# Two-layer graph network: the row of a node's mean from an on-chip table instead of a widened x; the dense pass beside the second and third mean pass

## The reference, cut to what matters

```python
def _sage_conv(x, src, dst, Wl, bl, Wr):
    summed = segment_sum(x[src], dst, N_NODES)
    cnt = segment_sum(ones, dst, N_NODES)
    mean = summed / maximum(cnt, 1.0)[:, None]
    return mean @ Wl.T + bl + x @ Wr.T
h = relu(_sage_conv(x, src, dst, Wl0, bl0, Wr0))
h = relu(_sage_conv(h, src, dst, Wl1, bl1, Wr1))
h = _sage_conv(h, src, dst, Wl2, bl2, Wr2)
x = layernorm(x + h)
# second layer: softmax attention of each edge over its source node
q, k, v = (x @ Wq)[src], (x @ Wk)[dst], (x @ Wv)[dst]
attn = einsum(q, (k + edges @ Wek) * scale) @ W_exp
attn = softmax of attn over the edges of one src
agg  = segment_sum(attn * (v + edges @ Wev), src)
x = layernorm(x + (x @ Wv - agg) @ W_out)
```

## Time and profile before

| | us |
|---|---|
| median of 3 runs | 3042.29 |
| lowest and highest | 3033.99, 3043.68 |
| span of the profiled execution | 3046.9 |

### The profile page before, as it was taken

How to read it: one execution, slowest core, us unless ns; L and a number is a source line. 1 busy time by engine, 2 the same in 40 slices (tenths; PEclk the granted TensorE clock), 3 DMA queues, 4 the chain that set the end, 5 groups by cost and what they waited for, 6 DMA issues and landing times.

```text
span 3046.9 us, 39880 instructions
## 1 busy us (share of the span) xinstructions
PE 1807.8 (59%) x8855; PEld 1270.6 (42%) x8855; DVE 1508.0 (49%) x4640; ACT 937.6 (31%) x2157; POOL 2059.0 (68%) x2154
## 2 busy tenths in 40 slices
PE   0159938994555556666666664777777777772000
PEld 0135525663444445544444443455555555551000
DVE  6767836883222223332333333577776776773000
ACT  0025524441111111112222221455655565552000
POOL 0037777776656557767777777777777777773776
PEclk9999969996777778787887876888988898986555
DMA  8954426886899967876434332344544445443221
GB/s 270 343 171 139 144 89 181 237 229 161 159 199 185 185 144 150 146 133 182 116 114 121 118 109 76 89 135 135 146 131 141 131 135 141 135 137 95 91 88 60
DMA packets 464252, 448.74 MB, mean 147 GB/s; under 512 B 62929, under 2 KB 342370, under 8 KB 464134
## 3 DMA queue, kind: packets, MB, share of 16 engines
q1 hardware_dynamic: 335558, 285.34, 30.9%
q0 software_dynamic: 62720, 110.02, 19.7%
q10 hardware_dynamic: 65856, 52.20, 5.2%
HBM read 285.01 MB, written 168.95 MB: 149 GB/s over the span
## 4 chain that ended last, share of the span: by engine, by line
POOL 39%; issue 27%; DMA 14%; PE 8%; DVE 8%; SPq 2%; POOLq 1%; ACT 1%; DVEq 0%; ACTq 0%
POOL GX L601 17%; POOL hsrc L601 10%; DMA dsti<-in_dst_dram 6%; POOL out_dram L677 4%; POOL x_with_lookup L616 4%; POOL x_prime L677 3%; DMA GX<-in_x_dram,idx_a 2%; PE bank L733 2%; PE bank L788 2%; DVE hsrc L1130 2%; DMA GX<-x_with_lookup,idx_a 1%; DVE hsrc L1131 1%; PE bank L792 1%; DMA GX<-mean_product,idx_a 1%; DMA x_prime<-normed,idx_b 1%
## 5 line engine op out<-in xcount | busy, mean ns | idle before, releaser
L601 POOL DMA_INDIRECT GX<-mean_product,idx_a x392 | 404.6, 1032 | 121.4 <-issue 109.2
L1265 DVE TENSOR_TENSOR_SCAN seg<-flag,seg,hsrc 128x512 f32<-128x512 f32 x147 | 188.7, 1284 | 523.0 <-ACT hsrc L975 421.6
L788 PE MATMUL bank<-h,wt 128*128 128x512 f32 x588 | 325.2, 653 | 0.8 <-ACT h L947 0.4
L825 PE MATMUL bank<-hsrc,wt 128*128 (+1 forms) x196 | 150.2, 858 | 254.4 <-ACT hsrc L975 134.0
L733 PE MATMUL bank<-ident,hsrc 128*128 128x128 f32 (+1 forms) x466 | 93.3, 336 | 320.0 <-DMA hsrc<-x_prime,idx_d 174.8
L733 PE MATMUL bank<-ident,GX 128*128 128x128 f32 x588 | 107.8, 313 | 286.2 <-DMA GX<-in_x_dram,idx_a 176.0
L601 POOL DMA_INDIRECT hsrc<-x_prime,idx_d x196 | 215.3, 1099 | 84.4 <-issue 44.8
L601 POOL DMA_INDIRECT hsrc<-x_prime,idx_c x196 | 209.8, 1070 | 59.7 <-issue 58.5
L601 POOL DMA_INDIRECT GX<-x_with_lookup,idx_a x196 | 209.9, 1071 | 58.8 <-issue 55.0
L677 POOL DMA_INDIRECT x_prime<-normed,idx_b x196 | 196.3, 1002 | 66.7 <-issue 63.8
L953 ACT ACTIVATE logv<-mv,eps 128x4 f32<-128x4 f32 x294 | 86.9, 296 | 487.7 <-DVE mv L1235 486.1
(11 more groups left out here) (164 smaller groups left out, 4403.4 us busy)
## 6 DMA issues: line engine op xcount, KB each, us to landing
flag<-same_dst_row SPq DMA_DIRECT2D x147, 256.0 KB
mean_product<-prod SPq DMA_DIRECT2D x147, 256.0 KB
hsrc<-mean_product SPq DMA_DIRECT2D x147, 256.0 KB, 3.7
x_with_lookup<-hsrc ACTq DMA_DIRECT2D x98, 264.0 KB, 4.6
hsrc<-in_x_dram ACTq DMA_DIRECT2D x98, 256.0 KB, 4.6
XN<-in_x_dram SPq DMA_DIRECT2D x98, 256.0 KB, 3.0
x_prime<-normed SPq DMA_DIRECT2D x98, 256.0 KB
XN<-x_prime SPq DMA_DIRECT2D x98, 256.0 KB, 4.8
```

The costliest lines, as they stand in the source:

```text
L601: pool.indirect_dma_start(buf[:, c.slot(U), t, 0:width], None, table, bass.IndirectOffsetOnAxis(ap=idx[:, c.slot(U), t:t + 1], axis=0)).th ...
L788: last = pe.matmul(psum[:, :], wt[:, T_R[i], :], before[:, c.slot(2), :], start=True, stop=not dst_phase)
L825: pe.matmul(psum[:, :], wt[:, T_R[i], :], take_cols(hsrc, c.index() * CH, CH), start=True, stop=False)
L1265: dve.tensor_tensor_scan(seg[:, c.slot(2), :], flag[:, c.slot(4), :], take_cols(hsrc, c.index() * CH, CH), seg[:, before.slot(2), CH - 1:C ...
```

## The change

1. **No widened tables.** `x_with_lookup`, `edge_attr_with_dst`, the phase lk and all that fed them are gone; mean0 gathers from x itself, attend from the edge values themselves.
2. **Marks.** During the sort ACT makes, for each of 200 columns of 125 destinations, two tiles of signs (256 and 196 wide, bf16), and PE sums their products in two banks, 400 matmuls in all (`mark`): a table of how many destinations lie below a node. 44 marks stand ahead of the first turn of the sort, up to 10 after each turn, and what is left (65) behind the turned indices. 8 buffers of marks.
3. **The table.** DVE and PE make from it `node_table`: for a node, the position of its mean, or a row of zeros (`make_table`, `table_sums`, put in by `run`'s new `middle`).
4. **Look-up in mean0.** For each chunk, DVE makes one-hot rows of the low byte (`look_hot_rows`), PE multiplies them by the table (`look_up`, 16 matmuls bf16 of 196), DVE picks by the high byte (`look_take`, 4 operations with a sum) and writes `lookup`. The mean part runs 6 chunks (`LAG`) ahead of it.
5. **Look-up in dst** of an edge's destination, in the same way, 8 matmuls bf16 of 256 and 4 picks of 256 a chunk, for `idx_d` of attend, whose wait and cast go.
6. **The dense pass** moves: chunks 0 to 48 beside mean1, 49 to 97 beside mean2, none beside mean0.
7. mean0's first gather waits only for the first turned list.

The core of the diff:

```diff
-            run(pe, "dense", chain, FIRST, to_end=False)
...
+            def look_up(c):
+                pe.wait_ge(look_hot.of(c), look_hot.after(c))
+                pe.wait_ge(look_done.of(c), look_done.after(c, 2 if c.phase == "mean0" else 1))
...
+                for t in range(TPC):
+                    to = bank[look_banks(c)[t // 2]][:, t % 2 * width:(t % 2 + 1) * width]
+                    for k, (rows, table) in enumerate(pairs):
+                        last = pe.matmul(to, rows[:, t * P:(t + 1) * P], table, start=k == 0, stop=k == len(pairs) - 1)
+                last.then_inc(look_sum.of(c), 1)
...
-                    run(pe, "mean0", [(3, second(chain_t), SECOND), (3, mean_turn), (2, second(chain_1), SECOND),
-                                      (1, mean_prod), (1, second(chain_2), SECOND), (0, second(chain_y), SECOND)], NC)
+                    run(pe, "mean0", [(LAG + 1, mean_turn), (0, look_up), (LAG, mean_prod)], NC, middle=table_sums)
+                    look_done.end(pe, "mean0")
                 else:
-                    run(pe, f"mean{i}", [(1, mean_turn), (0, mean_prod)], NC)
+                    dense = first if i == 1 else second
+                    run(pe, f"mean{i}", [(3, dense(chain_t)), (1, mean_turn), (2, dense(chain_1)),
+                                         (0, mean_prod), (1, dense(chain_2)), (0, dense(chain_y))], NC)
...
-            run(pe, "dst", chain, NC)
+            run(pe, "dst", [*chain, (8, look_up)], NC)
...
-                    run(dve, "mean0", [(3, mean_seg), (1, mean_scale), (1, second(add_x), SECOND),
-                                       (0, second(norm), SECOND)], NC)
+                    run(dve, "mean0", [(LAG + 1, mean_seg), (LAG, mean_scale), (1, look_hot_rows), (0, look_take)], NC,
+                        middle=make_table)
                 else:
-                    run(dve, f"mean{i}", [(1, mean_seg), (0, mean_scale)], NC)
+                    dense = first if i == 1 else second
+                    run(dve, f"mean{i}", [(1, mean_seg), (0, mean_scale), (1, dense(add_x)), (0, dense(norm))], NC)
...
-            run(dve, "dst", [(1, add_gathered), (0, norm)], NC)
+            run(dve, "dst", [(1, add_gathered), (0, norm), (9, look_hot_rows), (8, look_take)], NC)
...
-            run(pool, "lk", [(0, lk_settle), (4, block_of(lk_stage)), (3, lk_put)], NC)
...
+                gather(GX, ea, idx_a, c, ea_got)
+                gather(GP, xp, idx_c, c, gathered)
+                gather(GD, xp, idx_d, c, dst_got)
...
+            for f in range(MARK_TILES):
+                if f >= MARKS:
+                    act.wait_ge(mark_used, f - MARKS + 1)
+                act.activation(mark_a[0:MARK_ROWS, f % MARKS, :], count[0:MARK_ROWS, :], ACT.Sign, bias=mark_bias[0:MARK_ROWS, 0, f:f + 1])
+                act.activation(mark_b[0:MARK_ROWS, f % MARKS, 0:COLS], count[0:MARK_ROWS, 0:COLS], ACT.Sign,
+                               bias=mark_bias[0:MARK_ROWS, 1, f:f + 1]).then_inc(mark_made, 1)
```

More of the change, by code:

```diff
@@ L134, in run @@
         single(s)
+    if middle:
+        middle()
     with eng.Fori(0, whole) as j:
@@ L235, in gnn_kernel @@
         local = part([2, LINE])
-        value = part([8, LINE])
+        value = part([9, LINE])
+        ones = part([LINE])
+        step_i = part([WIDE], I32)
+        row_i = part([2], I32)
+        low = [part([LINE // 2], BF16) for _ in range(2)]
+        mark_i = part([2, MARK_TILES], I32)
+        mark_dst = part([MARK_TILES], I32)
         carry_row = sb("carry_row", [1, 3, P + 1])
@@ L537, in pl_load @@
                     sp.dma_start(PL[:, c.slot(U), i, :, :], sorted_rows(prod_table[i], c)).then_inc(pl_in.of(c), 16)
-            run(sp, "dst", [(0, pl_load)], NC)
+            run(sp, "dst", [(0, pl_load), (2, low_load)], NC)
             put_done.end(sp, "dst")
+            look_done.end(sp, "dst")
             def node_load(half):
@@ L630, in mean_stage @@
                 pool.wait_ge(m_turned.of(end), m_turned.after(end, U))
+                if c.phase == "mean1":
+                    more = BLOCK - 1 if not isinstance(c.j, int) else min(BLOCK, NC - c.index()) - 1
+                    pool.wait_ge(look_done.of(c), look_done.after(At("mean0", c.j, c.u + more)))
                 stage(c, idx_ready, (idx_a, col_i[:, V_SRC_A, :] if c.phase == "mean0" else lookup[:, :]))
@@ L691, in _ @@
             put_done.end(pool, "dst")
-            ea_out.end(pool, "mean1")
+            look_done.end(pool, "dst")
             def rows_used(c):
@@ L739, in _, with mark @@
                 turn_in(bank[2 + i // 4][:, i % 4 * P:(i % 4 + 1) * P], wraw[:, i, :]).then_inc(w_turned, 1)
+            marked = [0]
+            def mark(n):
+                for f in range(marked[0], min(marked[0] + n, MARK_TILES)):
+                    pe.wait_ge(mark_made, f + 1)
+                    for half in range(2):
+                        last = pe.matmul(bank[6 + half][:, 0:COLS], mark_a[0:MARK_ROWS, f % MARKS, half * P:(half + 1) * P],
+                                         mark_b[0:MARK_ROWS, f % MARKS, 0:COLS], start=f == 0, stop=f == MARK_TILES - 1)
+                    last.then_inc(mark_used, 1)
+                marked[0] = min(marked[0] + n, MARK_TILES)
+            mark(44)
             steps = turns = side = 0
@@ L752, in _, with value_turn @@
                 turns += 1
+                mark(10 if turns % 2 == 0 else turns // 2)
+            def value_turn(i):
+                if VALUE_AFTER[i]:
+                    pe.wait_ge(value_kept, VALUE_AFTER[i])
+                for a in range(2):
+                    last = turn_in(bank[VALUE_BANK[i]][:, a * P:(a + 1) * P], value[:, i, a * P:(a + 1) * P])
+                last.then_inc(value_turned, 1)
+            pe.wait_ge(value_ready, 1)
+            value_turn(V_SRC_A)
             pe.wait_ge(w_ready, 1)
@@ L849, in _ @@
             added.end(pe, "dst")
+            look_done.end(pe, "dst")
             def att_turn(i):
@@ L1254, in add_gathered @@
                 add(GX[:, c.slot(U), :, 0:D], c)
-            run(dve, "dense", [(1, add_x), (0, norm)], FIRST, to_end=False)
             def mean_seg(c):
```

345 lines of the change are left out of this document (216 added, 129 removed).

## The result

The changed kernel takes 3146.3 us (median of 4 runs, 3140.9 to 3151.3), the kernel before 3039.3 beside it (4 runs): a ratio of 1.035, interval 1.033 to 1.037. The change costs 3.5%. Its profiled execution has a span of 3139.1 us, 92.2 more than the 3046.9 of before.

The account below looks back on a forecast made before the run. POOL was taken to set the pace in lk, mean0, mean2, dst and attend, mean1 being the exception. Terms -247 + 51 + 126 + 193 - 46 = +77 on 3046.9 gave 3124, stated as 3120 us; range 3005 to 3215.

Parts of the forecast that it names:

- Part 1: Lk, sort and mean0: lk goes, last marks delay mean0, mean1's gathers start at 485 instead of 732.2: -247 us.
- Part 2: Mean1 and mean2 with 49 dense chunks each: 7.9 us a turn, +51 us in mean1 and +126 in mean2.
- The ring: Mean1 and mean2: DVE's addition, statistics, norm, scan, then PE's mean_prod to chain_y, wait for each other: 7.9 us a turn.
- the sentence on `dsti`: Mean1: ACT's 291.5 us wait for this tiny load was the exception there and goes with the change.
- Part 3: Dst: PE and DVE take turns because look_up waits for picks behind the addition; 15.4 us a turn, +193 us.
- the clock's share: Dst: PE's chain runs slower after each wait, taken as 2.3 us of the 15.4 us turn.
- The rule of the Trainium skill: Dst picks: an operation writing out its accumulator is two instructions; at a tenth of a us each, 16 us more.
- Part 4: Attend: a cast and part of a wait leave POOL's turn, 1.0 us x 49: -46 us.
- Rival A: Dst: PE keeps its full clock, turn 13.1 us, dst 623 us, kernel 3025 us; chance 0.15.
- B: Dst: POOL stays the pace at 10.6 to 11 us, picks and matmuls hidden, kernel 2925 us; chance 0.08.
- C: Mean1 and mean2: PE's clock falls to 0.82, turn 8.7 us, +80 us, kernel 3200 us; chance 0.12.
- D: Sort: marks hold it up, ACT over 1.05 us a mark, kernel up to 3150 us; chance 0.05.

Follow-up runs that it names:

- the third kernel: Changed kernel with leads of 2 in mean1 and mean2 and, in dst, DVE's look-up ahead of its addition: 2820.0 us, ratio 0.928.
- the kernel with the fill: Changed kernel with 52 unread PE transposes between chain_y and look_up in dst: 3076.8 us, ratio 1.012.

## Why the prediction was right, point by point

It forecast 3120 us, slower by 2.5%; measured were 3146.3 and 3.5%. Of the 26 us between them, 15 are in the stages (+92 instead of +77). The others lie in the step from profile to median: I took the median to be 4.6 us under the profiled time, and for the changed kernel it is 7 us above it.

**Part 1** (-247, measured -242.5). A mark took 0.747 us, not 0.77, and PE started mean0 at 229.3, not 238. Nearly 8 us of that come from an effect that I hadn't foreseen: the sort ended at 154.0 instead of 161.8, since DVE's wait for the keys ended 8.5 us earlier (0.9 us of that went into three new steps for the marks). The timeline of DVE, first of after and then of before:

```profile
12.18 0.27 DVE L1147 TENSOR_SCALAR hsrc<-hsrc 125x200 int32<-125x200 int32 x1 [3.03 <-DMA hsrc<-in_dst_dram]
```

```profile
20.72 0.29 DVE L1080 TENSOR_SCALAR hsrc<-hsrc 128x256 int32<-128x256 int32 x1 [16.43 <-DMA hsrc<-in_src_dram]
```

The copy of x no longer runs beside that load, the load is cut in other pieces, and SP issues it 1.2 us earlier; which of these did it wasn't separated. (POOL's first gather came at 156.6, 33 us before 189.5 and not 20, which won nothing, as it stalled behind chunk 6 all the same.) What was won by the earlier start of PE was lost in mean0, whose 42 chunks took 5.6 us each instead of 5.4, and at whose end POOL waited 16.5 us for the store instead of 14. The look-up is not the reason: after its stall POOL waited only 2.4 us for PE in the whole stage.

**Part 2** (+51 and +126, measured +61 and +136). The ring was read from the lists and priced from rows of before at 7.9 us; it is 7.91. Its parts are off by up to 0.1 us, with opposite signs: 4.49 us of DVE instead of 4.56, 3.42 of PE instead of 3.32. PE's wait, 1.5 us in the forecast, is 1.44. Undone, it gave 140 us back. Mis-sized were the ends of the stages: 32 and 22 us around the 49 turns, where I had 23 and 13. Right for the wrong reason was the sentence on `dsti`: the wait did go, but with the whole rewrite. The row that names it shows only which transfer came last. The DMA share of 0.92 in the earlier trace rows, beside 0.82 in mean2 of the same kernel, should have raised the question of the others, though it would not have settled it: in the third kernel mean1 has 0.96 with PE as its pace.

**Part 3** (+193, measured +187). DVE's part was forecast at 6.3 us and is 6.2 (1609.31 to 1615.53 in the changed kernel). PE's look-up at full clock is 1.03 us (forecast 1.1), the whole turn at full clock 12.7 (13.1), the clock's share 2.1 (2.3). So the turn of 14.78 is 0.6 under the forecast, 0.4 of it in the turn at full clock and 0.2 in the clock's share; but start and end of the stage took 105 us instead of 86. The two errors cancel within 6 us, and that is luck: the stage's total is nearer to the forecast than its parts.

The rule of the Trainium skill that the prediction weighed (VectorE: DVE Perf Modes, section "Two Vector instructions with no wait between them") agrees with the trace: it has a DVE_READ_ACCUMULATOR behind every pick, 392 in all, 0.08 us each. The cost that I had put on it does not: the next pick starts at the moment at which the read starts, every 0.40 us, and the 16 us that I had worked out from an assumed tenth of a us are not in the turn.

**Part 4** (-46, measured -50). As forecast: the cast and its wait are gone, and a turn in the middle of attend is 16.3 us (forecast 16.4).

**Rival A** (full clock in dst). It did not happen: 0.73. Its price was wrong on the more important side, though. I had 13.5 us a turn as the point below which the change gains. From the measured times that point is 14.78 - 107.0 / 41 = 12.2 us, and the kernel with the fill, at 12.7, is indeed still 1.2% slower than the kernel before (35 us, of which 22 are what the fill itself adds at the start of the stage). The whole ring had to go, not its clock. **B** was the better world but not this kernel's. **C** did not happen: the clock in the means was 0.97 with its wait of 1.44 us. **D** did not happen either: the sort ended 7.8 us earlier, not later.
